# A transformer layer with mixture of experts: the residual through TensorE, a new order of the front's steps, and shared chunks in other places

## The chip, the cores and the metric

The kernel runs on one core of a Trainium2 chip. The metric is the device time of one execution in microseconds (us). The engines are PE (TensorE), DVE (VectorE), ACT (ScalarE), POOL (GpSimd) and SP (SyncE, which here only issues transfers); they run side by side, each takes its own instructions in order, and semaphores make one wait for another.

## The reference

4 sequences of 1024 tokens with 128 features, all in float32. The first layer, and how its output enters the second, is:

```python
y = rmsnorm(x, norm_w)
y_conv = conv3(y, conv_w) + conv_b          # depthwise, along the tokens
h_t = tanh(a) * h_{t-1} + b * y_t           # scan along the tokens, y_ssm = h
x2 = x + y_conv + y_ssm
z = rmsnorm(x2, mlp_norm_w)
h = silu(z @ w_gate + b_gate) * (z @ w_up + b_up)       # 512 hidden features
x1 = layernorm(x + (x2 + h @ w_down + b_down))
```

The second layer is a mixture of 64 experts of width 88, of which each token takes 8, and a shared expert of width 176:

```python
scores = sigmoid(x1 @ gate_w.T)
choice = scores + gate_bias                 # 8 groups of 8 experts
group_scores = sum of the 2 largest choices of each group
masked = where(group is one of the 4 best, choice, 0)
topk_idx = top_k(masked, 8)                 # weights: scores there, to a sum of 2.5
routed = sum over the 8: weight * (silu(x1 @ Wg[e].T) * (x1 @ Wu[e].T)) @ Wd[e].T
shared = (silu(x1 @ Sg.T) * (x1 @ Su.T)) @ Sd.T
out = layernorm(x1 + routed + shared)
```

## The kernel before

The 4096 tokens are 32 tiles of 128, or 8 chunks of 512 (CT = 4 tiles in each). Three stages follow one another on PE.

**The front** goes in steps k = 0 to 8, written out by hand for each engine. In step k chunk k is in the first norm, the scan and the convolution, chunk k − 1 in the gated MLP, chunk k − 2 in the layer norm and the router, chunk k − 3 in the choice of experts and in its places. PE's part is `step(k)`: four `mlp_block`s (gate and up, two matmuls of 512 columns each, lines 595 and 596) of chunk k − 1; `transpose_x1` (628), `logits` (636), `ranks` (647 to 657) for the router; at the end of a batch `starts` (669 to 673) for the count of tiles of each expert; `mlp_base` (606 and 610), which puts the bias b_down and x2 into the bank OT; `square_sums` (587); four `mlp_down`s (616) that add to OT; then, for the next chunk, `spread` (557, it spreads a token's root over the partitions), `transpose_x` (548, into XT) and `transpose_y` (568, into OT). The end of the last `mlp_down` is the semaphore p_dn. DVE's `mlp_out` waits for it, adds x to OT (line 1277, s_v) and takes the statistics of the sum (1280); ACT's `root_v` (941) and `norm_v` (962) make x1 (s_x1r). ACT's `take_x` (982) copies the next chunk from XT with the convolution's bias and also waits for p_dn. `take_y` is line 970, `take_x1` 993, `silu` 989, the loads of the Silu and Sigmoid tables 1028, 1036 and 1038. DVE's `group_sums`, `compare_groups`, `mask_groups` and `choose` choose the experts, `take_ranks` gives each token its row in xs_dram (slots, line 1350), and POOL scatters the rows there (line 507).

**The routed experts** cover the first 28 tiles in two batches of 14. An expert gets one tile of rows for each 128 tokens that chose it, four such tiles are a quad, and a batch is 44 quads: SP loads the rows, PE transposes (803), multiplies (814), transposes (823) and multiplies again (834), and ACT stores to os_dram. SP's loads of a batch wait for all scatters of its tokens, PE's first transposition of it for these loads and for the shared chunks ahead (s_res). When a batch's outputs are stored, POOL gathers each token's 8 rows (line 512, 224 gathers over both batches), and DVE adds them with their weights (`add_round`, 1554). All scatters and gathers are in one queue on POOL.

**The shared expert** is done by chunks of 512 tokens (745, 746, then 765, and DVE's addition in line 1466). `SH_A` chunks stand ahead of batch 0, the chunks from `SH_A` to `SH_B` between the batches, the rest behind batch 1:

```python
SH_A, SH_B = 2, 3
```

**The dense part** comes last: the last chunk of 512 tokens goes through all experts by 44 products on PE (874, 875, 883), beside POOL's gathers of batch 1. In it `SUMS_IN_DENSE` says in which product DVE adds which set of gathered rows, `STATS_IN_DENSE` and `ROOT_AT` where the last layer norm of the chunks that are ready is done.

Of the kernel before, what the change touches and what calls it, by code (L numbers as in the profile page):

```python
# [77 lines left out]
SH_A, SH_B = 2, 3  # L78
# [44 lines left out]
V_NORM, V_CW, V_CB, V_A, V_B, V_MN, V_BG, V_BU = 0, 1, 4, 5, 6, 7, 8, 8 + NM  # L123
NV = 8 + 2 * NM
# [14 lines left out]
def build(nc, x, vecs, w_gate, w_up, w_down, b_down, gate_wT, gate_bias, wgu, wd, wdf, sgu, sd, out, xs, os):  # L139
    with ExitStack() as ctx:  # L140
# [86 lines left out]
        score = cut(CT, E)  # L227
# [11 lines left out]
        vr = cut(C)  # L239
# [297 lines left out]
        def _(pe):  # L537
# [1205 lines left out]
```

## Time and profile before

| | |
|---|---|
| median of 3 runs | 660.44 us (659.85 to 661.64) |
| the profiled execution | 660.38 us, of which 658.5 us are the span of the trace |
| busy: PE, DVE, ACT, POOL | 590.1, 460.9, 323.9, 448.2 us (90%, 70%, 49%, 68%) |
| first scatter, first gather, first gather of batch 1, last gather | 56.38, 355.10, 505.98, 649.38 us from the span's start |
| granted clock of TensorE, over the span | 0.962 of full speed |

Times inside the execution are counted from the start of the span. A busy share is a mean over stages of different kinds; PE's is high in all of them. A time in brackets behind an instruction is how long its engine stood idle ahead of it, and what ended that. "issue" is time in which an engine waited for nothing that the profile shows.

### The profile page before, as it was taken

Reading aid. Unit: us, or ns where it says so; the run is one execution under the profiler, and the core shown is the slowest. Engines: PE = TensorE matmul, PEld = TensorE weight load, DVE = VectorE, ACT = ScalarE, POOL = GpSimd, SP = SyncE. Lnnn points to the kernel's source line nnn. Section 1 sums busy time; section 2 is a strip of 40 time slices with the busy share of each in tenths; the row PEclk is TensorE's granted clock in tenths of the full one; section 3 lists DMA queues with packets and bytes.
Section 4 is the critical chain, followed back from the end, with each engine's and each line's share of the span. In section 5 each row is a group of like instructions: output and inputs, shape, how many; then the busy total and the mean of one; then the engine's idle time right before and its main releaser. Section 6 shows DMA issues by size and latency. Waiting matters only on the chain.

```text
span 658.5 us, 13356 instructions
## 1 busy us (share of the span) xinstructions
PE 590.1 (90%) x3456; PEld 472.7 (72%) x3457; DVE 460.9 (70%) x1311; ACT 323.9 (49%) x633; POOL 448.2 (68%) x464
## 2 busy tenths in 40 slices
PE   3976988888888999999997999999999999999980
PEld 2645656654555899999994999999995666666640
DVE  3456688878756889776773567677475598868785
ACT  8564876655553455455541445555552135253332
POOL 1004777777777777777776777777764777777773
PEclk9997999988997999999997899999999999999995
DMA  8962667651112687877754688888876123222122
GB/s 240 353 134 56 148 151 157 139 132 53 52 52 90 177 236 233 240 221 226 222 163 133 175 234 236 238 227 235 224 202 208 52 54 93 57 67 67 52 64 64
DMA packets 124605, 101.32 MB, mean 154 GB/s; under 512 B 15334, under 2 KB 114494, under 8 KB 124094
## 3 DMA queue, kind: packets, MB, share of 16 engines
q1 hardware_dynamic: 63766, 48.41, 27.6%
q0 software_dynamic: 14336, 29.39, 15.5%
q10 hardware_dynamic: 46464, 23.07, 12.2%
q8 instruction: 16, 0.26, 0.2%
q14 instruction: 23, 0.19, 0.1%
HBM read 52.58 MB, written 48.23 MB: 153 GB/s over the span
## 4 chain that ended last, share of the span: by engine, by line
PE 76%; DVE 9%; ACT 6%; issue 4%; POOL 3%; DMA 1%; POOLq 0%; DVEq 0%; ACTq 0%
PE GU L814 16%; PE OT L834 12%; PE XT L803 6%; PE HT L823 6%; PE OT L616 4%; PE GU L874 4%; PE GU L875 4%; PE XT L883 4%; PE GU L595 3%; PE GU L596 3%; POOL arena L512 3%; PE GU L745 2%; PE GU L746 2%; ACT x1r L962 2%; DMA arena<-os_dram,gslots 1%
## 5 line engine op out<-in xcount | busy, mean ns | idle before, releaser
L507 POOL DMA_INDIRECT xs_dram<-x1r,slots x224 | 227.6, 1016 | 121.8 <-issue 67.8
L512 POOL DMA_INDIRECT arena<-os_dram,gslots x224 | 218.4, 975 | 79.5 <-issue 66.7
L814 PE MATMUL GU<-wgu_sb,arena 128*128 x704 | 121.3, 316 | 0.1
L814 PEld LDWEIGHTS GU<-wgu_sb,arena 128*128 128x128 f32 x704 | 106.4, 192 | 0.8 <-issue 0.5
L834 PE MATMUL OT<-wd_sb,arena 88*128 x704 | 95.2, 278 | 1.7 <-ACT ol L1088 1.7
L1492 DVE TENSOR_TENSOR mlpw_sb<-GU,mlpw_sb 128x352 f32<-128x352 f32 x88 | 46.1, 524 | 67.8 <-ACT mlpw_sb L1078 61.2
L1088 ACT ACTIVATE ol<-OT 128x512 f32<-128x512 f32 x88 | 52.6, 597 | 83.1 <-PE OT L834 82.2
L834 PEld LDWEIGHTS OT<-wd_sb,arena 88*128 88x128 f32 x704 | 86.3, 193 | 3.6 <-issue 2.6
L1554 DVE SCALAR_TENSOR_TENSOR x_all<-arena,wk,x_all 128x128 f32<-128x128 f32 x224 | 66.3, 345 | 4.7 <-DMA arena<-os_dram,gslots 2.9
L1078 ACT ACTIVATE mlpw_sb<-GU 128x352 f32<-128x352 f32 x88 | 40.9, 464 | 48.7 <-PE GU L814 44.5
L1167 ACT ACTIVATE key<-GU 128x512 f32<-128x512 f32 x44 | 26.3, 597 | 69.9 <-PE GU L875 69.9
L1501 DVE COPY arena<-HT 88x512 f32<-88x512 f32 x88 | 59.6, 677 | 0.8 <-PE HT L823 0.8
L1071 ACT ACTIVATE arena<-XT 128x512 f32<-128x512 f32 x88 | 52.2, 593 | 9.6 <-PE XT L803 9.6
L803 PE MATMUL XT<-ident,arena 128*128 128x128 f32 x352 | 53.7, 275 | 2.4 <-ACT arena L1071 1.6
L823 PE MATMUL HT<-ident,mlpw_sb 128*88 128x128 f32 x352 | 52.9, 273 | 1.6 <-DVE arena L1501 1.6
L874 PE MATMUL GU<-x_all,wgu_sb 128*128 128x512 f32 x88 | 45.7, 601 | 1.5 <-DVE x1r L1466 0.9
L875 PE MATMUL GU<-x_all,wgu_sb 128*128 128x512 f32 x88 | 44.9, 592 | 0.0
L803 PEld LDWEIGHTS XT<-ident,arena 128*128 128x128 f32 x352 | 41.9, 143 | 3.5 <-issue 2.0
L823 PEld LDWEIGHTS HT<-ident,mlpw_sb 128*88 128x88 f32 x352 | 40.5, 122 | 4.5 <-DVE mlpw_sb L1492 1.6
L1592 DVE TENSOR_TENSOR key<-GU,key 128x512 f32<-128x512 f32 x44 | 30.2, 686 | 18.6 <-PE XT L883 10.3
L595 PE MATMUL GU<-arena,mlpw_sb 128*128 128x512 f32 x64 | 35.6, 640 | 7.9 <-DVE arena L1241 6.0
L874 PEld LDWEIGHTS GU<-x_all,wgu_sb 128*128 128x128 f32 x88 | 28.1, 327 | 17.4 <-issue 8.7
(205 smaller groups left out, 898.2 us busy)
## 6 DMA issues: line engine op xcount, KB each, us to landing
arena<-xs_dram SPq DMA_DIRECT2D x352, 64.0 KB
os_dram<-ol ACTq DMA_DIRECT2D x88, 256.0 KB
xs_dram<-ol SPq DMA_DIRECT2D x16, 512.0 KB, 4.4
wgu_sb<-wgu_dram SPq DMA_DIRECT2D x1, 5632.0 KB
xs_dram<-x1r,slots POOLq DMA_INDIRECT x224
arena<-os_dram,gslots POOLq DMA_INDIRECT x224
wd_sb<-wd_dram SPq DMA_DIRECT2D x1, 2816.0 KB
x_all<-x_dram SPq DMA_DIRECT2D x8, 256.0 KB, 5.7
```

What stands on the lines that cost most here:

```text
L507: g.indirect_dma_start(out=xs[b], out_offset=bass.IndirectOffsetOnAxis(ap=slots[:, t * K + k:t * K + k + 1], axis=0), in_=x1r[:, t, :], in ...
L512: return g.indirect_dma_start(out=gbuf[:, g_ % 2, t - SETS[g_][0], k, :], out_offset=None, in_=os[batch_of(t)], in_offset=bass.IndirectOff ...
L595: mm(GU[:, 2 * (m % 2), :], wgate_sb[:, m * P:(m + 1) * P], zT, start=True, stop=True)
L803: ins = tr(XT[:, i * P:(i + 1) * P], xl[:, u % 4, i * P:(i + 1) * P], ident[:, :])
L814: ins = mm(GU[:, 2 * r + i // 2, (i % 2) * 2 * I:(i % 2 + 1) * 2 * I], xg[:, r, i * P:(i + 1) * P], wgu_sb[:, bass.ds(at[i], 2 * I)], star ...
L823: ins = tr(HT[0:I, i * P:(i + 1) * P], eh[:, u % 2, i * I:(i + 1) * I], ident[:, :])
L834: ins = mm(OT[:, i * P:(i + 1) * P], hT[0:I, u % 2, i * P:(i + 1) * P], wd_sb[:, bass.ds(at[i], P)], start=True, stop=True)
L874: mm(GU[:, r, :], wgu_sb[:, j:E * 2 * I:I], x1T(NS), start=True, stop=True)
L875: mm(GU[:, r + 1, :], wgu_sb[:, HI + j:E * 2 * I:I], x1T(NS), start=True, stop=True).then_inc(p_dg, 1)
L1088: f(ol[:, u % 4, :], OT[:, :], ACT.Copy).then_inc(s_eo, 1)
L1501: v.tensor_copy(hT[0:I, u % 2, :], HT[0:I, :]).then_inc(s_ht, 1)
L1554: v.scalar_tensor_tensor(out=x_all[:, t, :], in0=gbuf[:, g % 2, t - SETS[g][0], kk, :], scalar=wk[:, t * K + kk:t * K + kk + 1], in1=x_all ...
```

## The change

The residual x no longer comes by DVE. ACT's `take_x` makes two copies from XT, one with the convolution's bias (x2T) and one with b_down (xbT, which is x + b_down), and `mlp_base` puts both into OT on PE: x2T by four transposes, xbT by four matmuls with the identity, in place of the bias matmuls over 512 columns. `mlp_out` and `norm_v` read OT itself. `spread` uses transposes in place of matmuls. `transpose_y` writes to XT from chunk 2 on and waits there for `take_x`. The steps of PE, ACT and DVE get another order, the scores go straight into rw, and `mask_groups` needs two operations for three. `SH_A, SH_B` become 4 and 6: four shared chunks ahead of batch 0, two between the batches, two behind. Of the last sums set 3 moves into the dense part, and one root and its norms move behind it.

On PE, step 4 from its start to the router's logits, before. zT (in arena) is the MLP's input, x1r the normed chunk; s_z, s_x1r, s_h, s_xT, s_yT, s_inv2 are inc'd as those are ready:

```order
L595 MATMUL GU<-arena,mlpw_sb 128x512 [waits s_z]
L596 MATMUL GU<-arena,mlpw_sb 128x512
L628 MATMUL XT<-ident,x1r 128x128 [waits s_xT,s_x1r]
L628 MATMUL XT<-ident,x1r 128x128 x3
L595 MATMUL GU<-arena,mlpw_sb 128x512 [waits s_z]
L596 MATMUL GU<-arena,mlpw_sb 128x512
L636 MATMUL MI<-gatew_sb,x_all 128x64 [waits s_x1T]
```

The same place of the changed kernel, whose lines 594, 595, 626 and 634 are 595, 596, 628 and 636 before, and 567 the transposition of y:

```order
L567 MATMUL XT<-ident,arena 128x128 [waits s_xT,s_yr]
L567 MATMUL XT<-ident,arena 128x128 x3
L594 MATMUL GU<-arena,mlpw_sb 128x512 [waits s_z]
L595 MATMUL GU<-arena,mlpw_sb 128x512
L594 MATMUL GU<-arena,mlpw_sb 128x512 [waits s_z]
L595 MATMUL GU<-arena,mlpw_sb 128x512
L626 MATMUL XT<-ident,x1r 128x128 [waits s_yT,s_x1r]
L626 MATMUL XT<-ident,x1r 128x128 x3
L634 MATMUL MI<-gatew_sb,x_all 128x64 [waits s_x1T]
```

Two blocks stand ahead of the transposition of x1, the logits right behind it, and ahead of it all the transposition of y now waits for `take_x` (s_xT).

On PE, the end of step 4, from the base on, before (lines 606 and 610 are the base, 587 the sums, 616 the downs, 557 the spread, 548 and 568 the transpositions of x and y):

```order
L606 MATMUL OT<-bdown_sb,ident 128x512 [waits s_yT]
L610 MATMUL OT<-ident,arena 128x128 x4
L587 MATMUL MI<-ones,arena 128x1 [waits s_root2,s_sc,s_sq2]
...
L616 MATMUL OT<-mlpw_sb,arena 128x128 [waits s_h]
...
L616 MATMUL OT<-mlpw_sb,arena 128x128 x3
L557 MATMUL GU<-ident,inv 128x128 [waits s_h,s_inv2]
L557 MATMUL GU<-ident,inv 128x128 x3
L548 MATMUL XT<-ident,x_all 128x128 [waits s_x1T,d_x5]
```

And in the changed kernel (605 and 608 are the base, 586 the sums, 614 the downs):

```order
L605 MATMUL OT<-ident,arena 128x128 [waits s_x1r]
L605 MATMUL OT<-ident,arena 128x128 x3
L608 MATMUL OT<-ident,arena 128x128 x4
L586 MATMUL MI<-ones,arena 128x1 [waits s_root2,s_sc,s_sq2]
...
L548 MATMUL XT<-ident,x_all 128x128 [waits s_x1T,d_x5]
...
L614 MATMUL OT<-mlpw_sb,arena 128x128 [waits s_h]
...
L557 MATMUL GU<-ident,inv 128x128 [waits s_h,s_inv2]
L557 MATMUL GU<-ident,inv 128x128 x3
L614 MATMUL OT<-mlpw_sb,arena 128x128 [waits s_h]
```

The transposition of the next x has moved ahead of the downs, the spread between the second and the third of them.

On ACT, the same step from `take_x` to `silu`, before (982 `take_x`, 970 `take_y`, 975 the neighbour chunk's column, 941 the root, 962 the norm, 1028 the Silu table, 993 `take_x1`, 989 `silu`):

```order
L982 ACTIVATE arena<-XT,vec 128x512 [waits p_dn,p_xT]
L970 ACTIVATE arena<-OT,vec 128x512 [waits s_x2,p_yT]
L975 ACTIVATE arena<-MI,vec 128x1 [waits p_yb]
L941 ACTIVATE root<-mv,eps 128x4 [waits s_mv]
L962 ACTIVATE x1r<-arena,nmean,inv 128x128 [waits s_inv3]
L962 ACTIVATE x1r<-arena,nmean,inv 128x128 x3
L1028 ACT_TABLE_LOAD
L993 ACTIVATE x_all<-XT 128x512 [waits p_x1]
```

And in the changed kernel:

```order
L984 ACTIVATE arena<-XT,vec 128x512 [waits p_dn,p_xT]
L985 ACTIVATE arena<-XT,vec 128x512
L972 ACTIVATE arena<-XT,vec 128x512 [waits s_x2,p_yT]
L943 ACTIVATE root<-mv,eps 128x4 [waits s_mv]
L1024 ACT_TABLE_LOAD
L964 ACTIVATE x1r<-OT,nmean,inv 128x128 [waits s_inv3]
L964 ACTIVATE x1r<-OT,nmean,inv 128x128 x3
L992 ACTIVATE arena<-GU,vec 128x512 [waits s_h,p_gu]
L996 ACTIVATE x_all<-XT 128x512 [waits p_x1]
```

`take_x` has a second operation, the table stands ahead of the norm, and the first `silu` ahead of `take_x1`.

The diff, cut to its core:

```diff
-SH_A, SH_B = 2, 3
+SH_A, SH_B = 4, 6
...
-SUMS_IN_DENSE = {4: (2, 2, 8), 5: (10, 1, 8), 6: (26, 1, 8), 7: (38, 1, 5)}
-STATS_IN_DENSE = {0: 0, 1: 1, 2: 2, 7: 3, 19: 4, 35: 5}
-ROOT_AT = (5, 21, 37)
+SUMS_IN_DENSE = {3: (0, 2, 8), 4: (7, 1, 8), 5: (20, 1, 8), 6: (36, 1, 8)}
+STATS_IN_DENSE = {0: 0, 1: 1, 2: 2, 15: 3, 28: 4}
+ROOT_AT = (5, 30)
...
+        def y_bank(k):
+
+            return OT if k < 2 else XT
...
-                    ins = mm(GU[:, 0, i * P:(i + 1) * P], inv[:, 1, t:t + 1].to_broadcast([P, P]), ident[:, :],
-                             start=True, stop=True)
+                    ins = tr(GU[:, 0, i * P:(i + 1) * P], inv[:, 1, t:t + 1].to_broadcast([P, P]), ident[:, :])
...
             def transpose_y(k):
                 pe.wait_ge(s_yr, k + 1)
                 if k >= 2:
-                    pe.wait_ge(s_v, k - 1)
+                    pe.wait_ge(s_xT, k + 1)
                 elif k:
                     pe.wait_ge(s_yT, k)
                 for i in range(CT):
-                    ins = tr(OT[:, i * P:(i + 1) * P], yr[:, i * P:(i + 1) * P], ident[:, :])
+                    ins = tr(y_bank(k)[:, i * P:(i + 1) * P], yr[:, i * P:(i + 1) * P], ident[:, :])
                 ins.then_inc(p_yT, 1)
...
             def mlp_base(c):
 
-                if c + 1 < NC:
-                    pe.wait_ge(s_yT, c + 2)
+                if c:
+                    pe.wait_ge(s_x1r, c)
                 else:
-                    pe.wait_ge(s_v, c)
-                if c == 0:
-                    pe.wait_ge(s_bd, 16)
-                mm(OT[:, :], ident[:, 0:1].to_broadcast([P, P]),
-                   bdown_sb[:, :].unsqueeze(1).to_broadcast([P, CT, P]), start=True, stop=False, skip_group_check=True)
+                    pe.wait_ge(s_yT, 2)
                 for i in range(CT):
                     tok = slice(i * P, (i + 1) * P)
-                    mm(OT[:, tok], x2T[:, c % 2, tok], ident[:, :], start=False, stop=False, skip_group_check=True)
+                    mm(OT[:, tok], x2T[:, c % 2, tok], ident[:, :], start=(i == 0), stop=False, is_transpose=True, skip_group_check=True)
+                for i in range(CT):
+                    tok = slice(i * P, (i + 1) * P)
+                    mm(OT[:, tok], xbT[:, c % 2, tok], ident[:, :], start=False, stop=False, skip_group_check=True)
...
             def transpose_x1(c, k):
                 pe.wait_ge(s_x1r, c + 1)
                 if k < NC:
-                    pe.wait_ge(s_xT, k + 1)
+                    pe.wait_ge(s_yT, k + 1)
...
+                last = CLAST.index(c - 1) if c - 1 in CLAST else None
                 if mlp:
                     mlp_block(k - 1, 0)
-                if route:
+                if c == EARLY:
                     transpose_x1(c, k)
-                if c == EARLY:
                     logits(c)
                 if mlp:
                     mlp_block(k - 1, 1)
-                if route and c != EARLY and c < ROUTED:
-                    logits(c)
+                if route and c != EARLY:
+                    transpose_x1(c, k)
+                    if c < ROUTED:
+                        logits(c)
+                if mlp:
+                    mlp_block(k - 1, 2)
                 if c >= 1 and c - 1 != EARLY and c - 1 < ROUTED:
                     ranks(c - 1)
                 if mlp:
-                    mlp_block(k - 1, 2)
-                if c - 1 in CLAST:
-                    starts(CLAST.index(c - 1))
+                    mlp_block(k - 1, 3)
+                if last is not None:
+                    starts(last)
                 if mlp:
-                    mlp_block(k - 1, 3)
                     mlp_base(k - 1)
                 neighbour(k + 1)
                 if c == EARLY:
-                    for m in range(NM // 2):
-                        mlp_down(k - 1, m)
+                    mlp_down(k - 1, 0)
+                    mlp_down(k - 1, 1)
                     ranks(c)
-                    for m in range(NM // 2, NM):
-                        mlp_down(k - 1, m)
                 if front:
                     square_sums(k)
+                if k + 1 < NC:
+                    transpose_x(k + 1)
                 if mlp and c != EARLY:
-                    for m in range(NM):
-                        mlp_down(k - 1, m)
-                if c - 1 in CLAST:
-                    tile_experts(CLAST.index(c - 1))
+                    mlp_down(k - 1, 0)
+                    mlp_down(k - 1, 1)
                 if front:
                     spread(k)
-                if k + 1 < NC:
-                    transpose_x(k + 1)
+                if mlp:
+                    mlp_down(k - 1, 2)
+                    mlp_down(k - 1, 3)
+                if last is not None:
+                    tile_experts(last)
                 if k and k + 1 < NC:
                     transpose_y(k + 1)
...
-                    ins = f(x1r[:, t, :], vr[:, i * P:(i + 1) * P], ACT.Identity, bias=nmean[:, t:t + 1],
+                    ins = f(x1r[:, t, :], OT[:, i * P:(i + 1) * P], ACT.Identity, bias=nmean[:, t:t + 1],
...
-                f(x2T[:, k % 2, :], XT[:, :], ACT.Identity, bias=vec[:, V_CB:V_CB + 1]).then_inc(s_xT, 1)
+                f(x2T[:, k % 2, :], XT[:, :], ACT.Identity, bias=vec[:, V_CB:V_CB + 1])
+                f(xbT[:, k % 2, :], XT[:, :], ACT.Identity, bias=vec[:, V_BD:V_BD + 1]).then_inc(s_xT, 1)
...
+                if route and k - 2 != EARLY:
+                    nc.scalar.preload_act_table(ACT.Silu)
+                if route:
                     norm_v(k - 2)
                 if k - 2 == EARLY:
                     nc.scalar.preload_act_table(ACT.Sigmoid)
                     take_x1(k - 2)
                     scores(k - 2)
+                if mlp and (not route or k - 2 == EARLY):
+                    nc.scalar.preload_act_table(ACT.Silu)
                 if mlp:
-                    nc.scalar.preload_act_table(ACT.Silu)
+                    silu(k - 1, 0)
                 if route and k - 2 != EARLY:
                     take_x1(k - 2)
                 if mlp:
-                    silu(k - 1, 0)
                     silu(k - 1, 1)
...
             def mlp_out(c):
 
                 dve.wait_ge(p_dn, c + 1)
-                v.tensor_tensor(vr, OT[:, :], flat(x_all[:, span(c), :]), ALU.add).then_inc(s_v, 1)
-                dve.wait_ge(s_v, c + 1)
                 for i in range(CT):
-                    ins = v.bn_stats(stats[:, i, :], vr[:, i * P:(i + 1) * P])
+                    ins = v.bn_stats(stats[:, i, :], OT[:, i * P:(i + 1) * P])
...
-                if c >= 1 and c - 1 != EARLY and c - 1 < ROUTED:
-                    choose(c - 1)
                 if c == EARLY:
                     group_sums(c)
                 if mlp:
                     hidden(k - 1, 0)
+                if c >= 1 and c - 1 != EARLY and c - 1 < ROUTED:
+                    choose(c - 1)
+                if mlp:
                     hidden(k - 1, 1)
...
+                if front:
+                    norm2(k)
                 if mlp:
                     mlp_out(k - 1)
-                if front:
-                    norm2(k)
                 if route and c != EARLY and c < ROUTED:
...
             add_shared(0)
+            shared_hidden(2, 0)
+            shared_hidden(2, 1)
             place_tiles(NBAT - 1)
             add_shared(1)
+            shared_hidden(3, 0)
+            shared_hidden(3, 1)
+            add_shared(2)
+            add_shared(3)
...
+            dve.wait_ge(s_acc, added(NS - 2))
+            mean_variance(tiles(NS - 2))
+            inverse_deviation(2)
```

## Rows read from the trace of the kernel before

**Rows 1.** Timeline of POOL: start, duration, engine, line, operation, out<-in, count [idle before <-releaser]
```profile
56.38 1.51 POOL L507 DMA_INDIRECT xs_dram<-x1r,slots  x1 [53.43 <-DVE slots L1350]
...
351.40 0.96 POOL L507 DMA_INDIRECT xs_dram<-x1r,slots  x1 [0.30 <-issue]
...
505.98 0.95 POOL L512 DMA_INDIRECT arena<-os_dram,gslots  x1 [4.68 <-issue]
...
649.38 0.94 POOL L512 DMA_INDIRECT arena<-os_dram,gslots  x1 [0.30 <-issue]
```

**Rows 2.** Chain that ended last, 645 to 658.5: start, us, what
```profile
649.38 2.71 DMA arena<-os_dram,gslots
```

**Rows 3.** Same chain, around the end of batch 0
```profile
350.93 1.71 PE GU L745 x2
...
360.91 0.67 PE XT L803 x4
```

**Rows 4.** Same chain, start of batch 0
```profile
213.90 0.67 PE XT L803 x4
```

**Rows 5.** Timeline of DVE: its addition of x at the ends of steps 5 to 8
```profile
124.28 0.69 DVE L1277 TENSOR_TENSOR arena<-OT,x_all 128x512 f32<-128x512 f32 x1 [2.21 <-PE OT L616]
...
149.49 0.69 DVE L1277 TENSOR_TENSOR arena<-OT,x_all 128x512 f32<-128x512 f32 x1 [2.42 <-PE OT L616]
...
172.18 0.69 DVE L1277 TENSOR_TENSOR arena<-OT,x_all 128x512 f32<-128x512 f32 x1 [1.78 <-PE OT L616]
...
191.18 0.69 DVE L1277 TENSOR_TENSOR arena<-OT,x_all 128x512 f32<-128x512 f32 x1 [1.59 <-PE OT L616]
```

**Rows 6.** Same chain, step 4
```profile
84.06 0.70 DVE arena L1277
...
88.24 1.66 ACT x1r L962 x4
...
89.94 0.65 PE XT L628 x4
...
97.41 0.86 PE OT L606 x2
...
98.27 0.89 PE OT L610 x8
...
99.95 3.69 PE OT L616 x32
...
103.73 0.70 DVE arena L1277
```

**Rows 7.** Same chain, shared chunks behind batch 1
```profile
504.05 1.78 PE OT L765 x16
...
509.27 1.79 PE XT L765 x16
```

**Rows 8.** Timeline of ACT, step 4
```profile
85.32 0.69 ACT L982 ACTIVATE arena<-XT,vec 128x512 f32<-128x512 f32 x1 [3.58 <-PE XT L548]
...
89.90 1.28 ACT L1028 ACT_TABLE_LOAD   x1
...
91.20 0.60 ACT L993 ACTIVATE x_all<-XT 128x512 f32<-128x512 f32 x1
```

**Rows 9.** Timelines of ACT (step 1) and PE (step 2)
```profile
34.19 0.26 ACT L936 ACTIVATE root<-MI,eps 128x4 f32<-128x4 f32 x1
...
63.51 2.08 PE L557 MATMUL GU<-ident,inv 128*128 128x128 f32 x8 [2.46 <-DVE inv L1237]
```

**Rows 10.** Groups by line and shape, DVE: count, busy us, mean ns, idle before
```profile
L1344 DVE TENSOR_TENSOR key<-HT,sel 128x256 f32<-128x256 f32 x7 | 2.9, 420 | 1.5 <-PE HT L657 0.8 <-PE HT L662 0.7
...
L1295 DVE TENSOR_TENSOR arena<-arena,gbias_sb 128x256 f32<-128x256 f32 x8 | 3.4, 421 | 4.1 <-ACT arena L1003 4.1
```

**Rows 11.** Timeline of PE, step 6
```profile
138.99 0.20 PE L669 MATMUL HT<-upto_bf,ntile_bf 64*128 64x64 bf16 x1 [2.22 <-DVE ntile_bf L1358]
```

**Rows 12.** Busy time of each engine in 84 to 104 (mostly step 4), with granted clock
```profile
84.00:104.00 20.00, 17.76 (x108) 12.81 (x107) 17.21 (x69) 13.93 (x24) 14.95 (x15) 1.00 0.64 148
```

More of the change, by code:

```diff
@@ L115 @@
 SUM_AT = {0: 60, 1: 68, 2: 80}
-SUMS_IN_DENSE = {4: (2, 2, 8), 5: (10, 1, 8), 6: (26, 1, 8), 7: (38, 1, 5)}
-STATS_IN_DENSE = {0: 0, 1: 1, 2: 2, 7: 3, 19: 4, 35: 5}
-ROOT_AT = (5, 21, 37)
+SUMS_IN_DENSE = {3: (0, 2, 8), 4: (7, 1, 8), 5: (20, 1, 8), 6: (36, 1, 8)}
+STATS_IN_DENSE = {0: 0, 1: 1, 2: 2, 15: 3, 28: 4}
+ROOT_AT = (5, 30)
 ROOTS = ((0, 3 * CT), (3 * CT, 5 * CT), (5 * CT, 6 * CT), (NST, NT), (NST - CT, NST - 1), (NST - 1, NST))
 ROOT_AFTER = (3, 5, 6, 7, 8, 9)
-V_NORM, V_CW, V_CB, V_A, V_B, V_MN, V_BG, V_BU = 0, 1, 4, 5, 6, 7, 8, 8 + NM
-NV = 8 + 2 * NM
+V_NORM, V_CW, V_CB, V_A, V_B, V_MN, V_BG, V_BU, V_BD = 0, 1, 4, 5, 6, 7, 8, 8 + NM, 8 + 2 * NM
+NV = 9 + 2 * NM
 M_LG, M_SS, M_YB = 0, 256, 264
@@ L136, in group_of, with build @@
     return max(g for g, (lo, hi) in enumerate(GROUPS) if lo <= c)
-def build(nc, x, vecs, w_gate, w_up, w_down, b_down, gate_wT, gate_bias, wgu, wd, wdf, sgu, sd, out, xs, os):
+def build(nc, x, vecs, w_gate, w_up, w_down, gate_wT, gate_bias, wgu, wd, wdf, sgu, sd, out, xs, os):
     with ExitStack() as ctx:
@@ L166, in build @@
         eps = sb("eps", [P, 2])
+        zero = sb("zero", [P, 1])
         ident = sb("ident", [P, P])
@@ L224, in cut @@
             return ap
-        score = cut(CT, E)
         choice = cut(CT, E)
@@ L238, in build @@
         h_sb = cut(NM, C)
-        vr = cut(C)
+        xbT = cut(2, C)
         xq = cut(C)
@@ L303, in build @@
         p_dn = sem("p_dn")
-        s_v = sem("s_v")
         s_mv = sem("s_mv")
@@ L753, in shared_down @@
                 elif c == 1:
-                    pe.wait_ge(s_v, NC)
+                    pe.wait_ge(s_x1r, NC)
                 else:
@@ L969, in take_y @@
                     act.wait_ge(s_x2, k - 1)
-                f(yT[:, k % 2, 1:C + 1], OT[:, :], ACT.Identity, scale=vec[:, V_NORM:V_NORM + 1]).then_inc(s_yT, 1)
+                f(yT[:, k % 2, 1:C + 1], y_bank(k)[:, :], ACT.Identity, scale=vec[:, V_NORM:V_NORM + 1]).then_inc(s_yT, 1)
             def take_neighbour(k):
@@ L1000, in scores @@
                 act.wait_ge(p_lg, c + 1)
-                if c:
-                    act.wait_ge(s_sel, c)
-                f(flat(score), MI[:, M_LG:M_LG + CT * E], ACT.Sigmoid).then_inc(s_sc, 1)
+                f(flat(rw[:, span(c), :]), MI[:, M_LG:M_LG + CT * E], ACT.Sigmoid).then_inc(s_sc, 1)
             row_squares(0)
@@ L1190, in _ @@
             nc.scalar.preload_act_table(ACT.Sqrt)
+            final_root(2)
+            act.wait_ge(s_ncmean, 3)
+            for t in range(*ROOTS[2]):
+                final_norm(t, t + 1 == ROOTS[2][1])
             final_root(3)
@@ L1219, in _ @@
             v.memset(eps[:, 0:1], RMS_EPS)
+            v.memset(zero[:, :], 0.0)
             v.memset(eps[:, 1:2], LN_EPS).then_inc(s_cdve, 1)
@@ L1294, in group_sums @@
                 dve.wait_ge(s_sc, c + 1)
-                then(v.tensor_tensor(choice, score, bc(gbias_sb[:, :].unsqueeze(1), P, CT, E), ALU.add))
+                then(v.tensor_tensor(choice, rw[:, span(c), :], bc(gbias_sb[:, :].unsqueeze(1), P, CT, E), ALU.add))
                 lo, hi = ch4[:, :, 0:EG // 2], ch4[:, :, EG // 2:EG]
@@ L1322, in mask_groups @@
                 n = CT * NG
-                then(v.tensor_scalar(m2, m1, GONE, None, ALU.is_equal))
-                then(v.tensor_tensor(ch4, ch4, bc(m2.unsqueeze(2), P, n, EG), ALU.mult))
-                then(v.tensor_scalar(choice, choice, 0.0, None, ALU.add))
+                then(v.tensor_scalar(m2, m1, GONE, None, ALU.not_equal))
+                then(v.copy_predicated(ch4, bc(m2.bitcast(U32).unsqueeze(2), P, n, EG),
+                                       bc(zero[:, 0:1].unsqueeze(2), P, n, EG)))
             def choose(c):
@@ L1337, in choose @@
                     dve.wait_ge(p_rank, c)
-                then(v.tensor_scalar(sel[:, ring(c), :], tab_a, GONE, None, ALU.is_equal))
-                v.tensor_tensor(rw[:, span(c), :], sel[:, ring(c), :], score, ALU.mult).then_inc(s_sel, 1)
+                if c == NS:
+                    then(v.tensor_scalar(sel[:, ring(c), :], tab_a, GONE, None, ALU.is_equal))
+                    v.tensor_tensor(rw[:, span(c), :], sel[:, ring(c), :], rw[:, span(c), :], ALU.mult).then_inc(s_sel, 1)
+                else:
+                    v.tensor_scalar(sel[:, ring(c), :], tab_a, GONE, None, ALU.is_equal).then_inc(s_sel, 1)
             def take_ranks(c):
@@ L1667, in _ @@
                     add_shared(c - 1)
-                    for k in range(3 * (c - SH_B - 1), min(K, 3 * (c - SH_B))):
-                        add_round(3, k)
             add_shared(NC - 1)
-            done_of = dict.fromkeys(range(4, NSET), 0)
+            done_of = dict.fromkeys(range(3, NSET), 0)
             for j in range(NJ):
@@ L1716 @@
     cols = [a("norm_w"), *a("conv_w")[:, 0, :].T, a("conv_b"), a("a"), a("b"), a("mlp_norm_w"),
-            *a("b_gate").reshape(NM, P), *a("b_up").reshape(NM, P)]
+            *a("b_gate").reshape(NM, P), *a("b_up").reshape(NM, P), a("b_down")]
     ins = {
@@ L1723 @@
         "w_down": a("w_down"),
-        "b_down": a("b_down"),
         "gate_wT": f("gate_w").T,
```

3 lines of the change are left out of this document (removed).

## The prediction

> **What bounds the kernel now.** I read the end first. The last indirect gather starts on POOL at 649.38 [rows 1], the chain that ended last goes from it into its own transfer of 2.71 us [rows 2] and then into sums and the last norm; 658.50 − 649.38 = 9.1 us lie behind that gather. The gathers of batch 1 start at 505.98, after POOL had stood idle for 4.68 us [rows 1]; the code makes the first of them wait until every expert output of batch 1 is stored. The other 111 follow in 143.4 us, 1.29 us each, against 0.94 + 0.30 in the last row. So the end is: start of those gathers + 143.4 + 9.1, and what starts them is the end of batch 1 on PE. The dense part on PE runs beside them.
>
> Next I followed PE backwards, to see what stands ahead of that end. Batch 1 starts at 360.91, after one shared chunk that begins at 350.93 [rows 3]. Batch 0 starts at 213.90 [rows 4]; its 137.0 us and batch 1's are dense PE work. Ahead lies the front, whose steps I cut at the end of their down projections, where DVE's add of x starts: 84.06, 103.73, 124.28, 149.49, 172.18, 191.18 [rows 5, 6]. Steps 4 and 5 take 19.7 and 20.6 us, step 6 takes 25.2, step 7 22.7, step 8 19.0. Scatters are a second line: POOL issues 224 of them from 56.38 to 351.40 [rows 1], 1.32 us each, and batch 1 can't start before the last has landed and been loaded.
>
> So **whatever lies on PE ahead of the end of batch 1 moves the end one for one; what lies behind it, beside the gathers, costs nothing.** That gives the change its sign: shared chunks move from behind to ahead.
>
> **Moved chunks, ahead of batch 0.** In a full stretch two chunks in turn are 504.05 and 509.27, 5.22 us apart [rows 7]. Two more ahead: +10.4. They could be free if batch 0 had to wait there for its scatters. The 112th scatter would be issued about 56.38 + 111 × 1.323 = 203.2; with an issue of 0.96, a landing as in [rows 2] and a load, for which I allow 2 to 3 us, batch 0 could start at 209 to 210. It starts at 213.90, so at most 4 us of PE's time there is cover.
>
> **Between the batches, two chunks for one.** The one chunk takes 350.93 to 360.91, 9.98 us: its blocks run at 1.71 us a pair [rows 3] where a pair of that width takes 0.86 elsewhere [rows 6], and its down projection waits for ACT and DVE. A second chunk's blocks (4 × 0.86) fit into that wait; then come its own down (1.8) and the add. I get 12.8 + 0.8 = 13.6 for 9.98, +3.6; the second chunk may also lift the pace of batch 1's first pairs, for which I take off 0.9: **+2.7**. Bounds: +1 (hidden in the wait but for its down) and +5.2.
>
> **Behind batch 1, three chunks fewer.** 15.7 us less on PE beside the gathers; the last gather doesn't move: nothing. The later sums and the later root 2 fall into the same stretch; set 7's gathers still come last. Bounds: DVE keeps up better and gathers go gapless, (1.29 − 1.24) × 111 = −5; or an add too many behind the last gather, +1. I take 0, since the buffers' releases come from DVE work that is only moved.
>
> **The front, a usual step.** From x1r on PE runs without a gap [rows 6]: from 89.94 to 103.6, 13.7 us, the down projections (99.95, 3.69) being last. What changes behind x1r:
> - one pair more stands ahead of the transposition of x1, so blocks 0 and 1 run beside the norm: −1.72.
> - the base: 0.86 (the bias, two records of 512 columns) + 0.89 (x2T, four matmuls in eight records [rows 6]) become four transposes (four records, half of 0.89) and four matmuls: 1.33 for 1.75, −0.4.
> - the logits now wait for ACT's copy with nothing between: +0.6 (a 512-column ACT operation takes 0.69 [rows 8], the pitch is less).
> - the transposition of x(k+1) and the spread now stand ahead of the last downs: four records each, +0.44 and +0.44 (the spread had eight before, 2.08 at the low clock in [rows 9]).
>
> The sum is −0.64. Ahead of x1r, what is late next is take_x. It still waits for the downs, has two ACT operations now (from 0.69 to 1.3 us, [rows 8]), and on PE transpose_y waits for both, with blocks 0 and 1 queued behind it. DVE's add (0.70, the row at 84.06) goes, but the norm starts at 88.24 [rows 6] behind ACT's root, and that root stands behind take_x and take_y. The Silu table (1.28 [rows 8]) goes from behind the norm to ahead of it, where the wait for DVE's mean covers it. So x1r ends 5.9 us after the downs, as before. Handovers that are new on PE cost some 0.35 of the 0.64: I take **−0.3 for step 4 and −0.5 for step 5**. Bounds for each: −1.5 and +1, as DVE, busy for most of a step, may not follow.
>
> Its batch-norm statistics read PSUM now. A 256-column DVE operation takes 420 ns from PSUM and 421 ns from SBUF [rows 10], so I cost this at nothing. [...]
>
> **The front, steps that differ.**
> - Steps 1 to 3. ACT's root of the mean squares starts at 34.19 [rows 9], late because of ACT's queue; the spread waits for it, and downs 2 and 3 now stand behind the spread, so step 1 ends at 36.6 for 34.73: +1.9. At 63.51 [rows 9] the spread begins where step 2's downs have long been done; behind it and at the low clock downs 2 and 3 put that step's end at +5.3. Step 3 gets 2.0 of this back, since that spread and transposition now lie ahead of the cut: **+3.3**. The first scatter comes about 1.3 later. Bounds: 0 and +5.3.
> - Step 6. PE stands 2.22 us for the tile counts [rows 11], and the pairs behind go at half pace. The new order puts block 3 ahead of that wait: 25.2 becomes 22.2, **−3.0** (bounds 0 and −4.1).
> - Step 7 begins with DVE's table work ahead of the norm and has a slow stretch like it; with two blocks ahead of x1r: **−2.8** (0 and −3.5).
> - Step 8 has no take_x and no next transposition: −1.72 − 0.4 + 0.6 − 0.7 (the add, which was on its path): **−2.3**. The add is gone from the last norm as well: **−0.6**.
>
> Together 3.3 − 0.3 − 0.5 − 3.0 − 2.8 − 2.3 − 0.6 = **−6.2** for the front; with the bounds it lies between −14 and 0.
>
> **Sum.** −6.2 + 10.4 + 2.7 = +6.9 at the end of batch 1, nothing behind it. The profiled execution took 660.38 (span 658.50 and 1.88 around it), the median of the runs 660.44: no difference to speak of. **660.4 + 6.9 = 667.3 us.**
>
> **Rivals.**
> 1. *The front gains much more, and the new chunks fill a wait for scatters.* If the front shortens by over 13.1, the end moves ahead. For it: in 20 us of step 4 PE is busy for 17.76 and DVE for 17.21 [rows 12], and steps 6 and 7 are longer still. Against: the loop downs, take_x, transposition, norm, x1 is kept. Its floor is POOL: batch 0 not before 209.5 (−4.4), and 2.7 between gives 658.7; if the first scatter also comes a little earlier than now, 657 to 658. It decides from a front shorter by 15.
> 2. *The front gains nothing, or loses.* Transpose_y, behind two ACT operations, heads PE's queue, so PE stands for some 1.3 us a step just there, and pairs of 1.71 us for 0.86 stand right behind batch 0's last quad [rows 3]. Then the gains of steps 6 and 7 go into slow pairs, the front gives about 1, and the time is 672. [...]
> 3. *No change that can be told.* Front −11 to −13 (early steps cost nothing, step 4 and 5 give 1.5 each), or −9 and gapless gathers: 659 to 662.
>
> **Chances.** My forecast (665 to 670) 0.42; rival 2 (670 and over) 0.20; between the forecast and rival 3 (662.4 to 665) 0.10; rival 3 0.12; rival 1 0.16. About 0.3%, 2 us, is what a measurement here can tell from no change: faster 0.16, same 0.12, slower 0.72. For 8 in 10 the range goes down into rival 1's floor and up over rival 2's 672: 658 to 673.5. The forecast's own is 665 to 670.
>
> **What would show it.** Right: batch 0's first transposition near 218, batch 1's near 368, its first gather near 513, the last near 656; cuts of steps 4 and 5 still 19 to 20 us apart, step 6 near 22; PE waiting for ACT ahead of transpose_y; the dense part ending near 633 (15.7 less than 6.9 later than now) with POOL still gathering for over 20 us. Wrong: batch 0 starting at 210 behind a DMA (rival 1), or pairs of 1.7 us in every step (rival 2). I am wrong in mechanism if the time between the first and the last gather of batch 1 changes by over 3 us.

## The result and the profile after

The changed kernel takes 668.36 us (median of 4 runs, 667.62 to 668.58) against 660.99 of the kernel before in the same comparison: ratio 1.010, 95% interval 1.0075 to 1.0125. It is slower by 7.4 us; the forecast was 667.3, +6.9. The profiled execution took 668.58, its span is 666.8. The sum was right, several of its terms were not, and their errors cancelled.

POOL after, in the columns of [rows 1]; the third row is the first gather of batch 1, the last row the last gather:

```profile
62.32 1.51 POOL L507 DMA_INDIRECT xs_dram<-x1r,slots  x1 [59.36 <-DVE slots L1361]
...
358.17 1.01 POOL L507 DMA_INDIRECT xs_dram<-x1r,slots  x1 [0.30 <-issue]
...
515.24 0.94 POOL L512 DMA_INDIRECT arena<-os_dram,gslots  x1 [0.30 <-issue]
...
657.74 0.94 POOL L512 DMA_INDIRECT arena<-os_dram,gslots  x1 [0.30 <-issue]
```

The last gather is 8.4 later than in [rows 1], and the span is 8.3 longer, so the time is lost ahead of it. The scatters began 5.9 later, for a forecast of 1.3. The chain that ended last, from the norm of the last chunk to the start of batch 1:

```profile
195.54 1.15 ACT x1r L964 x3
...
223.30 0.67 PE XT L805 x4
...
358.21 1.15 PE OT L836 x8
359.36 0.86 PE GU L747 x2
...
370.99 0.67 PE XT L805 x4
```

Batch 0 starts 9.4 later than in [rows 4], batch 1 10.1 later than in [rows 3]. The front itself ended as it did before (the norm of the last chunk begins at 195.19; before, at 194.71). Where its gain went is seen at the cuts. DVE's statistics take the place of the addition in [rows 5, 6]; steps 1 to 8:

```profile
39.70 0.89 DVE L1288 BATCH_NORM_STATS2 stats<-OT 128x6 f32<-128x128 f32 x4 [1.04 <-PE OT L614]
...
74.01 0.89 DVE L1288 BATCH_NORM_STATS2 stats<-OT 128x6 f32<-128x128 f32 x4 [2.67 <-PE OT L614]
...
92.71 0.89 DVE L1288 BATCH_NORM_STATS2 stats<-OT 128x6 f32<-128x128 f32 x4 [0.97 <-PE OT L614]
...
113.86 0.89 DVE L1288 BATCH_NORM_STATS2 stats<-OT 128x6 f32<-128x128 f32 x4 [0.97 <-PE OT L614]
...
133.82 0.89 DVE L1288 BATCH_NORM_STATS2 stats<-OT 128x6 f32<-128x128 f32 x4 [0.97 <-PE OT L614]
...
156.49 0.89 DVE L1288 BATCH_NORM_STATS2 stats<-OT 128x6 f32<-128x128 f32 x4 [0.97 <-PE OT L614]
...
175.87 0.89 DVE L1288 BATCH_NORM_STATS2 stats<-OT 128x6 f32<-128x128 f32 x4 [0.96 <-PE OT L614]
...
192.37 0.89 DVE L1288 BATCH_NORM_STATS2 stats<-OT 128x6 f32<-128x128 f32 x4 [1.14 <-PE OT L614]
```

At the end of step 3 the front stands 8.6 behind ([rows 6]: 84.06), at the end of step 4 10.1; from there it regains 9 us in steps 5 to 8. PE in steps 1 and 2 shows two things: it waits for DVE's inverse root ahead of the spread, with half the down projections behind it, and it runs slowly.

```profile
22.38 1.92 PE L595 MATMUL GU<-arena,mlpw_sb 128*128 128x512 f32 x2
24.09 1.91 PE L594 MATMUL GU<-arena,mlpw_sb 128*128 128x512 f32 x2
25.79 1.29 PE L595 MATMUL GU<-arena,mlpw_sb 128*128 128x512 f32 x2
26.92 1.02 PE L594 MATMUL GU<-arena,mlpw_sb 128*128 128x512 f32 x2
...
37.23 0.65 PE L557 MATMUL GU<-ident,inv 128*128 128x128 f32 x4 [1.57 <-DVE inv L1247]
...
48.53 2.02 PE L594 MATMUL GU<-arena,mlpw_sb 128*128 128x512 f32 x2
...
69.44 1.11 PE L557 MATMUL GU<-ident,inv 128*128 128x128 f32 x4 [1.51 <-DVE inv L1247]
70.35 3.62 PE L614 MATMUL OT<-mlpw_sb,arena 128*128 128x128 f32 x16
```

A pair of 512 columns takes 1.9 where the same pair takes 1.02 a little later; I call that half pace. Sixteen records of the down projections take 3.62 at 70.35, where 32 take 3.69 in [rows 6]. In the view by windows (length, busy time and count of PE, PEld, DVE, ACT and POOL, granted clock, DMA share, GB/s) the stretch in step 2 is:

```profile
48.70:54.00 5.30, 5.30 (x8) 1.97 (x8) 3.11 (x10) 3.04 (x4) 0.00 (x0) 0.54 0.00 2
```

A granted clock of 0.54 is near the 0.50 that the same view gives at the end of this step, from 69.00 to 74.00. Before, the blocks of step 2 (46.50 to 54.00) had 1.00. In step 1 the same view gives 1.00 throughout, from 22 to 28 us, although the pairs take 1.9 there: for step 1 the half pace is read from the durations alone, and that the clock caused it is not shown.

### The profile page after: what moved, and what is told of

It reads as the page before. It is cut to its first block, busy times and chain, and to the rows that moved or that the text cites. A ratio compares the mean times of both kernels' runs of the same rounds, so it can differ in the third digit from the quotient of the medians.

```text
span 666.8 us, 13300 instructions
## 1 busy us (share of the span) xinstructions
PE 582.8 (87%) x3440; PEld 467.2 (70%) x3441; DVE 452.1 (68%) x1289; ACT 325.1 (49%) x639; POOL 446.4 (67%) x464
## 4 chain that ended last, share of the span: by engine, by line
PE 77%; ACT 8%; DVE 8%; issue 4%; DMA 1%; POOL 1%; POOLq 0%; DVEq 0%; SPq 0%; ACTq 0%
PE GU L816 16%; PE OT L836 12%; PE XT L805 6%; PE HT L825 6%; PE GU L876 5%; PE XT L885 5%; PE GU L877 5%; PE OT L614 4%; PE GU L594 3%; PE GU L595 2%; PE GU L747 2%; PE GU L748 2%; DVE x_all L1572 2%; ACT x1r L964 1%; ACT arena L927 1%
## 5 line engine op out<-in xcount | busy, mean ns | idle before, releaser
L876 PEld LDWEIGHTS GU<-x_all,wgu_sb 128*128 128x128 f32 x88 | 28.2, 327 | 19.5 <-issue 9.9
L594 PE MATMUL GU<-arena,mlpw_sb 128*128 128x512 f32 x64 | 38.2, 683 | 0.9 <-DVE arena L1251 0.9
```

The source lines that it names most:

```text
L594: mm(GU[:, 2 * (m % 2), :], wgate_sb[:, m * P:(m + 1) * P], zT, start=True, stop=True)
L876: mm(GU[:, r, :], wgu_sb[:, j:E * 2 * I:I], x1T(NS), start=True, stop=True)
```

## The experiments

"Before" is the kernel before in the same comparison. The front's end is the start of the last chunk's norm. The five columns on the right are read from each kernel's one profiled execution.

| kernel | us, median | before | ratio, 95% interval | first scatter | front's end | batch 0 | batch 1 | last gather |
|---|---|---|---|---|---|---|---|---|
| before | | 660.99 | 1 | 56.38 | 194.71 | 213.90 | 360.91 | 649.38 |
| changed | 668.36 | 660.99 | 1.010 (1.0075 to 1.0125) | 62.32 | 195.19 | 223.30 | 370.99 | 657.74 |
| E1 | 665.37 | 661.34 | 1.0056 (1.0042 to 1.007) | 59.59 | 193.20 | 216.14 | 363.46 | 653.83 |
| E2 | 669.58 | 661.34 | 1.0124 (1.0086 to 1.0162) | 58.15 | 194.57 | 223.82 | 371.21 | 658.32 |
| E3 | 662.99 | 661.34 | 1.002 (1.0 to 1.0039) | 58.57 | 185.90 | 215.35 | 365.90 | 652.75 |
| E4 | 664.82 | 661.34 | 1.006 (1.0037 to 1.0083) | 59.25 | 191.32 | 217.74 | 365.59 | 652.96 |
| E5 | 660.60 | 661.87 | 0.9987 (0.9967 to 1.0007) | 56.67 | 186.15 | 212.57 | 360.25 | 648.17 |
| E6 | 668.26 | 661.87 | 1.0093 (1.0063 to 1.0122) | 60.99 | 193.36 | 221.48 | 371.80 | 658.49 |
| E7 | 661.34 | 661.87 | 0.9988 (0.9972 to 1.0004) | 58.33 | 185.52 | 211.06 | 361.59 | 650.42 |
| E8 | 662.09 | 661.87 | 1.0002 (0.9987 to 1.0018) | 58.73 | 186.04 | 210.44 | 362.35 | 649.74 |
| E9 | 660.68 | 661.11 | 0.9995 (0.9981 to 1.0009) | 57.48 | 185.38 | 213.50 | 359.57 | 648.47 |

**E1, the front alone.** The changed front, everything behind it as before:

```diff
-SH_A, SH_B = 4, 6
+SH_A, SH_B = 2, 3
-SUMS_IN_DENSE = {3: (0, 2, 8), 4: (7, 1, 8), 5: (20, 1, 8), 6: (36, 1, 8)}
+SUMS_IN_DENSE = {4: (2, 2, 8), 5: (10, 1, 8), 6: (26, 1, 8), 7: (38, 1, 5)}
...
```

> The changed front with the shared chunks and the sums as before (two ahead, one between, five behind). Theory A (what lies on PE ahead of the end of batch 1 sets the time; the changed front gains nothing in all, x1r of the last chunk came at 195.2 for 194.7): batch 0 starts at 214 to 215, the time is 660 to 662. Theory B (the front costs 8 us, since its first scatter came 6 us later and POOL's scatters hold batch 1 back): 664 to 668, with batch 1's first transposition waiting for a DMA. Theory C (the later sums cost the time): 660 or less, and the kernel with the chunks alone at about 660 too.

665.37, 4.0 more than before, though its front ended 1.5 earlier. That is theory B, which I had as the rival. PE's first transpositions of batch 0 and of batch 1:

```profile
216.14 1.08 PE L805 MATMUL XT<-ident,arena 128*128 128x128 f32 x4 [5.33 <-DMA arena<-xs_dram]
...
363.46 1.09 PE L805 MATMUL XT<-ident,arena 128*128 128x128 f32 x4 [1.77 <-DMA arena<-xs_dram]
```

PE was free for batch 0 5.33 earlier, but its rows had not come: the scatters had begun 3.2 late. So PE's queue isn't the only bound. In the changed kernel the two chunks more ahead of batch 0 hide this wait: PE waits for no DMA there, nor inside batch 0.

**E2, the chunks alone.** The old front with the new places of chunks and sums:

```diff
-SH_A, SH_B = 2, 3
+SH_A, SH_B = 4, 6
...
+            shared_hidden(2, 0)
+            shared_hidden(2, 1)
             place_tiles(NBAT - 1)
```

> The front as before with four shared chunks ahead, two between, two behind, and the later sums. Theory A: batch 0 starts 9 to 10 us later than before (223 to 224), batch 1 10 to 12 later, the time is 668 to 670, as of the whole change. Theory B (the front costs the time, the chunks fill a wait for scatters): 660 to 662.

669.58, +8.2: theory A. Batch 0 starts 9.9 later, batch 1 10.3 later, the last gather 8.9 later. The moved chunks with the later sums make the whole loss, without the new front. The sums were not run by themselves, but theory C has nothing left to explain: the last gather is late by what batch 1 is late, less 1.4.

**E3, the old order in steps 0 to 2:**

```diff
-                if front:
+                if front and k > 2:
                     spread(k)
                 if mlp:
                     mlp_down(k - 1, 2)
                     mlp_down(k - 1, 3)
+                if front and k <= 2:
+                    spread(k)
```

(and DVE's `norm2` behind `mlp_out` in the same steps).

> The changed kernel with the old order in steps 0 to 2 alone: the spread behind all down projections, DVE's norm2 behind mlp_out. Theory A1 (the early steps lose because downs 2 and 3 wait behind the spread for ACT's root): p_dn of step 1 at about 36.5 for 39.7, of step 2 at about 65 for 74.0, x1r of the second chunk some 5 us earlier, the time 662 to 664. Theory A2 (they lose because PE runs at half pace there): downs end earlier, but the pairs behind keep 1.7 us, the time moves by less than 2 us: 666.5 to 668.

662.99, within A1's range; step 2 ends at 67.21, though, for the 65 that A1 gave. PE in steps 1 and 2:

```profile
33.30 3.74 PE L614 MATMUL OT<-mlpw_sb,arena 128*128 128x128 f32 x32
36.88 0.60 PE L557 MATMUL GU<-ident,inv 128*128 128x128 f32 x4
...
63.98 3.19 PE L614 MATMUL OT<-mlpw_sb,arena 128*128 128x128 f32 x16
67.01 0.60 PE L557 MATMUL GU<-ident,inv 128*128 128x128 f32 x4
```

No wait is left ahead of the spread; the downs of step 2 still run at half pace, but they do so while ACT works on the root. Step 2 ends 6.8 earlier than in the changed kernel (67.21 for 74.01), the front 9.3 earlier; the other 2.5 are slow pairs in steps 4 and 6 that this execution doesn't have (more of them under E6).

**E4, spare PE work.** 57 transpositions of the identity that nobody reads:

```diff
+                if k == 1:
+                    spare(5)
                 if mlp:
                     mlp_block(k - 1, 0)
                 if c == EARLY:
+                    spare(6)
                     transpose_x1(c, k)
+                    spare(8)
                     logits(c)
...
+                if c == EARLY:
+                    pe.wait_ge(s_h, NM * k)
+                    spare(38, GU[:, 3, :])
```

> The changed kernel with 57 transpositions of the identity more on PE, in the stretches where it stands in steps 1 and 2 (5 ahead of block 0 of step 1, 6 and 8 around the transposition of x1 in step 2, 38 ahead of its sums); their results are not used. Theory A2 (half pace): the pairs of step 1 and step 2 take 0.86 for 1.7 us, the first scatter comes at 56 to 58 for 62.3, the front ends 6 to 8 us earlier, the time is 660 to 663. Theory A1: more PE work where PE waits changes nothing or costs a little: 668 to 669.

664.82; the time fell by 2.6 us by the ratios and 3.5 by the medians, less than A2 expects, where A1 expects no gain. PE:

```profile
19.25 1.27 PE L683 MATMUL HT<-ident 128*128 128x128 f32 x5
...
22.17 1.71 PE L595 MATMUL GU<-arena,mlpw_sb 128*128 128x512 f32 x2
23.71 1.02 PE L594 MATMUL GU<-arena,mlpw_sb 128*128 128x512 f32 x2
...
66.37 1.12 PE L557 MATMUL GU<-ident,inv 128*128 128x128 f32 x4 [2.78 <-DVE inv L1258]
67.28 3.62 PE L614 MATMUL OT<-mlpw_sb,arena 128*128 128x128 f32 x16
```

Step 1's pairs are at 1.02 from 23.71 on, for 26.92 in the changed kernel (24.91 in E1, whose step 1 has the same code); but ahead of the spread PE still stands, 2.78 us, and the downs behind it still run at half pace. Both losses exist, and the spread's place is the larger. One execution each would not show that, for step 2 ends at 74.01, 71.28 and 72.62 in the changed kernel, E1 and E6, which have the same code up to there; but it ends at 67.21, 66.84 and 67.37 in the three with the old order alone (E3, E7, E8), at 70.94 with the spare work alone (E4), and at 63.93 and 64.73 with both (E5, E9).

**E5, both.** E3 and E4 together.

> The changed kernel with both: the old order in steps 0 to 2, and the 57 spare transpositions. If waiting behind the spread and half pace are two losses, they add: first scatter near 57 (58.6 and 59.3 in the two alone), x1r of the last chunk near 184 (185.9 and 191.3), the time 1 to 2 us below the first alone. If they are one loss (PE's waits for the spread make the half pace), the spare work finds nothing left to mend after step 1 and the time is that of the old order alone within 1 us.

660.60, by the ratios 0.33% below E3, some 2 us, little more than the intervals of the two. The first scatter comes at 56.67, 5.65 earlier than in the changed kernel, for 3.75 and 3.07 in the two alone; the front's end, 186.15, is no earlier than E3's, and the 184 expected is missed. Step 3 takes 20.54 here for E3's 18.70, and step 8 takes 18.19 for 16.50, both with slow pairs. This is the changed kernel with its early steps mended, and it takes what the kernel before takes.

**E6, the logits behind block 2** from step 3 on:

```diff
                 if route and c != EARLY:
                     transpose_x1(c, k)
-                    if c < ROUTED:
-                        logits(c)
                 if mlp:
                     mlp_block(k - 1, 2)
+                if route and c != EARLY and c < ROUTED:
+                    logits(c)
```

> The changed kernel with the logits behind block 2 from step 3 on, so that PE doesn't stand while ACT copies x1. Theory A3 (the 0.6 us wait ahead of the logits also takes the pace: block 2 takes 3.2 for 1.7 us in steps 4 and 6): the front ends 3 to 5 us earlier, the time is 664 to 666. Rival: the scores, and DVE's group sums behind them, come 1.7 us later and hold the end of the step: 668 to 670.

668.26, no change, where A3 gave 664 to 666. PE in step 4:

```profile
97.52 0.66 PE L626 MATMUL XT<-ident,x1r 128*128 128x128 f32 x4 [0.50 <-ACT x1r L964]
98.98 1.10 PE L594 MATMUL GU<-arena,mlpw_sb 128*128 128x512 f32 x2 [0.80 <-DVE arena L1281]
```

And in the changed kernel:

```profile
100.09 1.10 PE L634 MATMUL MI<-gatew_sb,x_all 128*128 128x64 f32 x8 [0.69 <-ACT x_all L996]
101.03 1.64 PE L594 MATMUL GU<-arena,mlpw_sb 128*128 128x512 f32 x2
102.46 1.91 PE L595 MATMUL GU<-arena,mlpw_sb 128*128 128x512 f32 x2
```

At the same place PE now waits 0.80 for DVE's first hidden block, where the changed kernel waits 0.69 for ACT's x1. One wait has taken the other's place, and the pair behind it keeps its pace. That is not E6's doing: E1, E3, E4, E5, E7, E8 and E9 have the wait of 0.69 too, and step 4 takes 19.45 or 19.46 in all of them, for 21.15 in the changed kernel's one profiled execution. Step 6 is slow in the changed kernel and E1 (22.67 and 22.66) and takes 21.87 to 21.90 in the others. So A3 falls: the wait alone doesn't take the pace. The late scores do no harm either (the cuts of step 4 are 19.5 apart, as in E1). The front's end 1.8 earlier than in the changed kernel was lost between the batches, at half pace.

**E7, E3's front with the old chunks and sums.**

> The changed front with the old order in steps 0 to 2, and the chunks and sums as before (two ahead, one between, five behind). Theory A alone (PE ahead of the end of batch 1): the front ends 8.8 us earlier than before, so the time is 651 to 653. With POOL's scatters as a second bound (batch 0 not before the 112th scatter + 6.9, batch 1 not before the last + 6.7): batch 0 at 210, batch 1 at 358 to 360, both behind a DMA, and the time is 656 to 659.

661.34, the same as before within 0.3%, where PE's queue alone gave 651 to 653 and the second bound 656 to 659: both are missed. The front ends 9.2 us earlier than before, and nothing comes of it:

```profile
211.06 1.09 PE L807 MATMUL XT<-ident,arena 128*128 128x128 f32 x4 [6.66 <-DMA arena<-xs_dram]
213.02 1.11 PE L807 MATMUL XT<-ident,arena 128*128 128x128 f32 x4 [0.87 <-DMA arena<-xs_dram]
213.92 2.50 PE L818 MATMUL GU<-wgu_sb,arena 128*128 x8
```

and in the chain, the first shared pair behind batch 0 and the first transposition of batch 1:

```profile
351.54 1.71 PE GU L749 x2
...
361.59 0.67 PE XT L807 x4
```

Batch 0 starts 2.8 earlier than in [rows 4] and ends 0.6 later than in [rows 3]: it takes 140.5 us for 137.0, and that is what the second bound's 656 to 659 leaves out. Behind its start PE waits for rows twice more (1.3 us in all), and behind the wait of 6.66 it runs slowly: the granted clock is 0.50 from 211.0 to 214.0 and 0.55 from there to 216.5. Batch 1's first transposition waits for no DMA, unlike expected.

**E8, three ahead, one between,** with E3's front and the later sums of the changed kernel:

```diff
-SH_A, SH_B = 4, 6
+SH_A, SH_B = 3, 4
```

> The same front with three shared chunks ahead of batch 0 and one between, four behind, and the later sums. Theory A alone: 5.2 us more than with two ahead. With the scatters as a second bound: the third chunk fits into the wait for the scatters, batch 0 at 210 to 211, batch 1 at 358 to 361, the time that of two ahead within 1 us, 656 to 659, and below the kernel before by some 2 us.

662.09, 0.8 above E7 and equal to before: the third chunk is free, as the scatters' bound has it. The gain over before that I expected (656 to 659) did not come; batch 0 starts at 210.44 and then waits for rows in the chain, 2.14 us of it PE's, and runs at a granted clock of 0.55 to 0.56 from 213.0 to 220.7:

```profile
213.41 3.94 DMA arena<-xs_dram
217.40 1.12 PE XT L807 x4
```

**E9, E5 with one chunk between the batches** (`SH_A, SH_B = 4, 5`).

> The kernel with the old order in steps 0 to 2 and the spare transpositions, with one shared chunk between the batches for two (four ahead, three behind). By PE's queue alone batch 1 ends 3 to 5 us earlier than with two between and the time is 656 to 658. By the scatters (POOL's last one still starts near 351.3, and the loads behind it take their time) PE reaches batch 1 earlier but waits there for loads, batch 1 ends at 494 to 496 as with two between, and the time is within 1 us of it: 659.5 to 661.5.

660.68, with E5's ratio inside its interval: the scatters' bound again. The chain from POOL's last scatter to batch 1:

```profile
351.11 3.60 DMA xs_dram<-x1r,slots
...
357.06 2.26 DMA arena<-xs_dram
...
359.57 1.10 PE XT L818 x4
```

PE stood 2.95 us ahead of that row. A chunk less between the batches leaves a wait in its place, and batch 1 starts 0.7 earlier than in E5.

## Why the prediction was right, and where it was not

**The mechanism was right for this change, but it is one of two.** More work on PE ahead of the end of batch 1 moves the end, and what lies behind it costs nothing: E2 shows the first half, and the changed kernel's last dense product starts at 634.09, 6.7 earlier than before, with 23.6 us of gathers still to come, the second (forecast: near 633). "One for one" does not hold the other way: in E7 the front is 9.2 shorter and the time the same, and in E1 it is 1.5 shorter and the time 4.0 longer, since the scatters came later. The prediction had the scatters as "a second line" and gave them at most 4 us. The last dense product, after and before:

```profile
634.09 1.12 PE L885 MATMUL XT<-key,ol 128*128 128x512 f32 x2 [0.72 <-DVE key L1612]
```

```profile
640.75 1.12 PE L883 MATMUL XT<-key,ol 128*128 128x512 f32 x2 [1.65 <-DVE key L1594]
```

**The chunks** ahead were put at +10.4. From the last norm to batch 0 there are 28.1 us for 19.2: +8.9. Between the batches I took +2.7; it is 11.63 for 9.98, +1.65, because the last down projections of batch 0 and the pairs behind ran at full pace this time (1.15 and 0.86, [rows 3]: 1.71). E3 and E6, with the same chunks, ran there at half pace and took 13.3 us. The batches themselves were 1.0 and 1.6 shorter, the wait for the stores and the delayed last gathers of batch 0 cost 0.8 more, and the gathers ran 0.9 faster.

**The front was wrong as a whole**: −6.2 forecast, +0.5 measured. (The bounds of its steps come to −13.5 and +4.4, not to the −14 and 0 that the prediction states, and the terms of step 8 to −2.2.) Its usual steps were sized well: step 5 −0.6 (−0.5), step 6 −2.5 (−3.0), step 7 −3.3 (−2.8), step 8 −2.5 (−2.3), the last norm −0.7 (−0.6). Step 4 took +1.5 for −0.3, as its block 2 ran at half pace; in the other executions (under E6) it took −0.2, as forecast. The step that failed is **"Steps 1 to 3: +3.3"**: it was +8.6, above my upper bound of 5.3, and +8.4 in E1. I had the spread's wait in it, but took the root itself as it was before; in step 1, behind the blocks at half pace, the root came 2.5 later (36.70 for 34.19 in [rows 9]), and in step 2 it came 5.9 later, with the downs behind it at half pace (the low clock of [rows 9] is a granted clock of 0.50, from 63.50 to 67.00; it is 0.50 from 69.00 to 74.00 in the changed kernel). ACT's root in the changed kernel, and before in step 2:

```profile
36.70 0.26 ACT L938 ACTIVATE root<-MI,eps 128x4 f32<-128x4 f32 x1
...
68.91 0.26 ACT L938 ACTIVATE root<-MI,eps 128x4 f32<-128x4 f32 x1
```

```profile
62.98 0.26 ACT L936 ACTIVATE root<-MI,eps 128x4 f32<-128x4 f32 x1
```

E3 shows the place of the spread as the larger cause, E4 and E5 the pace as the smaller. How the pace falls differs between executions of one code: E1, with the front of the changed kernel, kept its pace in the blocks of step 2 (a granted clock of 1.00 from 48.70 to 54.00, for 0.54) and scattered first at 59.59. Even E2, whose front is the one before, scattered first at 58.15 for 56.38. So the parts are sure to 2 us only.

**That the sum came so close is luck.** At the last gather the front is 6.7 us worse than forecast, and the other terms together 5.2 better: the chunks 1.5 and 1.05, the batches 1.0 and 1.6, the gathers 0.9, less the 0.8 for the stores. So +6.9 became +8.4 there, and +7.4 in the medians.

**Rival 2** came true in part: the front gave nothing, with half pace in steps 1, 2, 4 and 6, not in every step, but the time stayed below its 672.

**Rival 1 was priced wrongly.** I let batch 0 start at 209.5 and then run its 137 us. E7 and E8 start it at 210 to 211, but the rows behind the first come no faster than SP loads them (E7: eight loads take 4.03 us), and the first quads run at half pace behind the wait; batch 0 ends 0.6 (E7) and 1.4 (E8) later than before. So the kernel before stood close to both bounds, PE's queue and the scatters with their loads, and a shorter front by 9 us is worth nothing by itself. With that seen, 0.16 for "faster" was too much.

**What didn't matter, as forecast:** the statistics from PSUM take 285 ns for 281 ns from SBUF over 32 operations each, so 4 ns more each. And the table ahead of the norm cost its load alone:

```profile
116.88 1.28 ACT L1024 ACT_TABLE_LOAD   x1
118.18 1.51 ACT L964 ACTIVATE x1r<-OT,nmean,inv 128x128 f32<-128x128 f32 x4
```

The next operation stands 0.02 us behind it.

No version beat both kernels: E5, E7, E8 and E9 are level with the kernel before. Whether an earlier first scatter would do it is not shown: none came before that kernel's own 56.38, E5's 56.67 being the nearest.

## What to carry to other kernels

Before moving work ahead of a stage to fill a wait, look whether the stage waits for data at all, and then at the second bound that lies close behind: here PE's queue and POOL's scatters stood within a few us of each other, so shortening one alone gave nothing and lengthening one cost its full size. Price the first steps of a pipeline by their own rows; engines that wait there for long chains can turn a reorder that is nearly free in the steady state into the largest term of the front (here +8.6 in steps 1 to 3, and −0.2 to −0.6 in steps 4 and 5). A bound on "when the stage may start" is not a bound on when it ends: ask at what rate its inputs come behind the first, and at what pace the engine runs behind the wait.

## What the runs showed of the hardware

PE ran at half pace behind some waits. With four records for eight in the spread, and the spread moved behind the transposition of x, next to a wait of 0.93 us, the pairs of step 1 ran at 1.9 for 1.02 us; which of these did it is not separated, and the granted clock reads 1.00 there. Five spare transpositions of 1.27 us in all brought the pace back earlier: the pairs are at 1.02 from 22.0, 23.7 and 23.7 us on in E5, E4 and E9, and from 24.9 to 26.9 in the changed kernel, E1, E3, E6, E7 and E8, which lack them. Behind the wait of 6.66 us in E7 the granted clock was 0.50 (211.0 to 214.0), for 1.00 ahead of it (200 to 204 us), and the first quad's products took 2.50 us for 1.36 two quads later, so this wait for rows cost more than its own length.

Whether PE keeps its pace over a short wait varies between executions of one code, and was worth 1 to 3 us each time: the blocks of step 2 in the changed kernel and in E1 (its end at 74.01 and at 71.28); the wait of 0.69 us in step 4, behind which only the changed kernel's profiled execution was slow (21.15 us for 19.45); the end of batch 0 in the changed kernel and in E3 (a granted clock of 1.00 from 356 to 363 us, and of 0.50 from 350 to 356; 11.63 and 13.3 us between the batches).
